# Row-tiled attention with keys and queries in one tile of three places: eight transfers a turn for fourteen, and another order of the sync queue's turn

## What is computed

```python
def attention(query, key, value, mask):         # query is layernorm(x), key and value are ctx
    q = split_heads(query @ Wq.T + bq)           # 16 heads of 8
    k = split_heads(key @ Wk.T + bk)
    v = split_heads(value @ Wv.T + bv)
    scores = einsum('bhqd,bhkd->bhqk', q, k) / sqrt(8)
    scores = where(mask, finfo.min, scores)
    return merge(softmax(scores) @ v) @ Wo.T + bo

x = x + tanh(g_xattn) * attention(layernorm(x), ctx, ctx, mask)
x = x + tanh(g_ffn) * experts(layernorm(x))      # softmax gate less a threshold, gelu, two layers each
```

## Time and profile before

| what | us |
|---|---|
| median of three runs | 675.66 |
| the profiled execution | 676.67 |
| its span, first to last instruction | 674.9 |
| PE busy (share of the span) | 613.6 (91%) |
| DVE busy | 496.8 (74%) |
| ACT busy | 377.8 (56%) |
| POOL busy | 175.8 (26%) |
| mean granted clock of TensorE | 0.944 |

### The profile page before, as it was taken

One profiled execution on the slowest core, in us unless ns is written; L12 is line 12 of the kernel. 1 busy time (PEld: TensorE's weight loads), 2 busy tenths in 40 slices (PEclk: granted clock), 3 DMA queues, 4 the chain that ended last, 5 costly groups with the idle time before them and its releaser, 6 DMA issues.

```text
span 674.9 us, 13858 instructions
## 1 busy us (share of the span) xinstructions
PE 613.6 (91%) x4480; PEld 464.6 (69%) x4480; DVE 496.8 (74%) x926; ACT 377.8 (56%) x620; POOL 175.8 (26%) x223
## 2 busy tenths in 40 slices
PE   5798889889888988749999999999999999999998
PEld 4655556556566655437878878878788788787886
DVE  4447787685766676555888888888888888888886
ACT  2134444454544444517766766767667666676673
POOL 5423333333434223210121221221212212212121
PEclk8769898897988899959999999999999999999999
DMA  5545454454543432004112111111112121111110
GB/s 155 180 132 146 130 150 135 131 152 119 159 122 115 124 120 63 3 1 70 48 48 63 48 47 63 48 47 62 47 48 60 47 62 47 47 62 47 46 63 16
DMA packets 50879, 55.14 MB, mean 82 GB/s; under 512 B 10768, under 2 KB 37264, under 8 KB 50832
## 3 DMA queue, kind: packets, MB, share of 16 engines
q1 hardware_dynamic: 50672, 54.51, 27.9%
q10 hardware_dynamic: 160, 0.00, 0.0%
HBM read 39.16 MB, written 14.81 MB: 80 GB/s over the span
## 4 chain that ended last, share of the span: by engine, by line
PE 73%; SPq 10%; DMA 7%; issue 3%; ACT 3%; DVE 2%; POOL 1%; DVEq 0%; ACTq 0%
PE ps_h L1086 9%; PE ps_y L1066 9%; PE ps_y L1067 9%; PE ps_y L1068 9%; PE ps_h L1088 9%; PE ps_h L1087 9%; DMA mask_words<-in_mask 5%; PE scores L872 4%; SPq L401 3%; PE misc L935 3%; SPq L393 3%; SPq L384 2%; PE scores L890 2%; PE misc L863 2%; PE misc L961 2%
## 5 line engine op out<-in xcount | busy, mean ns | idle before, releaser
L618 ACT ACTIVATE h_sb<-ps_h,b_sb 128x512 f32<-128x512 f32 x256 | 176.3, 690 | 109.0 <-PE ps_h L1088 95.6
L823 DVE TENSOR_TENSOR h_low<-h_sb,h_high 128x512 fp32r<-128x512 f32 x256 | 164.3, 682 | 0.0
L819 DVE CAST h_high<-h_sb 128x512 fp32r<-128x512 f32 x128 | 98.5, 770 | 68.5 <-ACT h_sb L618 68.5
L506 POOL TENSOR_TENSOR yT<-yT,weighted 128x512 f32<-128x512 f32 x54 | 69.7, 1291 | 301.8 <-DVE weighted L811 301.8
L648 DVE TENSOR_REDUCE neg_max<-scores 128x8 f32<-128x1024 f32 x64 | 77.8, 1221 | 50.6 <-PE scores L872 50.5
L1086 PE MATMUL ps_h<-x_high,w_high 128*128 (+1 forms) x256 | 102.9, 402 | 2.3 <-ACT h_sb L618 1.6
L1066 PE MATMUL ps_y<-h_high,w_high 128*128 128x512 f32 x256 | 101.6, 397 | 0.8 <-DVE h_low L823 0.8
L1067 PE MATMUL ps_y<-h_low,w_high 128*128 128x512 f32 x256 | 101.4, 396 | 0.0
L1068 PE MATMUL ps_y<-h_high,w_low 128*128 128x512 f32 x256 | 101.1, 395 | 0.0
L1088 PE MATMUL ps_h<-x_high,w_low 128*128 (+1 forms) x256 | 100.0, 391 | 0.0
L1087 PE MATMUL ps_h<-x_low,w_high 128*128 (+1 forms) x256 | 99.9, 390 | 0.0
(11 more groups left out here) (124 smaller groups left out, 783.0 us busy)
## 6 DMA issues: line engine op xcount, KB each, us to landing
w_row<-w_scratch SPq DMA_DIRECT2D x64, 256.0 KB, 3.1
kq_scratch<-kq_high SPq DMA_DIRECT2D x64, 128.0 KB, 2.6
k_st<-kq_scratch SPq DMA_DIRECT2D x64, 96.0 KB
q_st<-kq_scratch SPq DMA_DIRECT2D x64, 96.0 KB
w_raw<-in_w_ffn SPq DMA_DIRECT2D x16, 256.0 KB, 2.9
kq_scratch<-kq_low SPq DMA_DIRECT2D x32, 128.0 KB, 2.1
ctx_sb<-in_ctx SPq DMA_DIRECT2D x16, 128.0 KB, 2.4
out_y<-y_out SPq DMA_DIRECT2D x7, 256.0 KB, 2.3
```

The costliest lines, as they stand in the source:

```text
L618: nc.scalar.activation(h_sb[:, j % HBUF, :], ps_h[:, j % 4, :], ACT.Gelu_apprx_tanh, bias=b1_sb[:, j:j + 1]).then_inc(h_done, 1)
L819: V.tensor_copy(h_high[:, j % HBUF, :], h_sb[:, j % HBUF, :]).then_inc(high_odd, 1)
L823: V.tensor_tensor(h_low[:, j % HBUF, :], h_sb[:, j % HBUF, :], h_high[:, j % HBUF, :].bitcast(F32), ALU.subtract).then_inc(low2_done, 1)
```

## The change

Keys and queries now lie in one tile `kq_st` with three places (group g in g % 3), each row with keys and queries side by side. One load of 24 x 2048 takes both, so four loads stand for eight. ScalarE and VectorE write four parts into `kq_parts` in the order k_low, q_high, k_high, q_low, so that two neighbours are one combination and one store of 32 x 4 x 512 takes both; with two high stores of 32 x 4 x 256 that makes four stores for six. The bytes are the same. The copies of the max rows, two for each b, stay as they are but for their target.

SP's turn has another order: max rows of b = 1, x, ctx, w_raw, the mask (now of the group after the next, `group_at(it, 2)`), loads of kq, max rows of b = 0, high stores, low stores. The wait for a free place looks three groups back. The second norm's scaling (L712, now L734) moves on VectorE from behind `kq_low` to behind `inT_low`. `headsT` and `x_biased` have one place instead of two, and their writers wait for the group before.

At the start, ctx of group 1 is loaded earlier, six loads of weights and biases (`later_weights`) come behind the first kq loads, group 0's two low stores are issued by ScalarE (`first_low_stores`), the V weights' split (`first_weights`) comes behind group 0's kq parts on both engines, and the nine idle matmuls before group 0's scores become two there and one, two or three at four other points (before group 0's and group 1's kq matmuls, group 0's first max transpose and V's matmuls); the nine at the very start stay.

```diff
-        k_st = sa("k_st", [P, 2, SLABS, GT], F32R)
-        q_st = sa("q_st", [P, 2, SLABS, GT], F32R)
-        kq_high = sa("kq_high", [P, 2, 2, GT], F32R)
-        kq_low = sa("kq_low", [P, 2, 2, GT], F32R)
+        kq_st = sa("kq_st", [P, 3, SLABS, 2, GT], F32R)
+
+        kq_parts = sa("kq_parts", [P, 2, 4, GT], F32R)
...
+            sp.dma_start(ctx_sb[:, 1, :, :], ctx_v[1]).then_inc(ctx_in[1], 16)
             sp.dma_start(wv_raw, a["wvT"]).then_inc(wts_early_in, 16)
...
+            def later_weights():
+
+                sp.dma_start(bo_row[:], a["bo"].partition_broadcast(P)).then_inc(wts_in, 16)
...
+            def rows_of(g, c):
+                return kq_dram[g].rearrange("(r c d) (s x) -> c (d s) r x", r=ROWS, c=3, s=SLABS)[c]
...
-                    for n, c in ((0, 1), (1, 2)):
-                        store(n, c, kq_low[:, u, n, :], g, low_stored[u])
...
+                    if g > 0:
+                        wait_count(sp, mask_done, g - 1)
+                        sp.dma_start(mask_words[:, u, :, :], mask_v[g]).then_inc(mask_in[u], 16)
+                if (g := group_at(it, 1)) is not None:
+                    u = g % 2
...
+                    sp.wait_ge(high_stored[u], g // 2 * 32 + 32)
+                    sp.wait_ge(low_stored[u], g // 2 * 32 + 32)
+                    wait_count(sp, tr_low_full, 2 * (g - 3) + 2)
+                    for r in range(ROWS):
+                        sp.dma_start(kq_st[32 * r:32 * r + 24, g % 3, :, :, :].rearrange("p s n t -> p (s n t)").bitcast(F32),
+                                     kq_dram[g, 24 * r:24 * r + 24, :]).then_inc(kq_in[g % 3], 16)
+                    if g == 0:
+                        later_weights()
+                if (g := group_at(it, 0)) is not None:
+                    misc_wait_read(sp, "max0", g)
+                    wait_count(sp, tr_low_full, 2 * (g - 3) + 1)
...
-                    for n, c in ((0, 0), (0, 2), (1, 0), (1, 1)):
-                        store(n, c, kq_high[:, u, n, :], g, high_stored[u])
+                    for n in range(2):
+                        sp.dma_start(rows_of(g, 0)[:, :, n * GT:(n + 1) * GT], kq_parts[:, u, 2 - n, :].bitcast(F32)).then_inc(high_stored[u], 16)
+                    if g > 0:
+                        misc_wait_read(sp, "kq", g)
+                        for c in (1, 2):
+                            sp.dma_start(rows_of(g, c), kq_parts[:, u, 2 * c - 2:2 * c, :].rearrange("p n t -> p (n t)").bitcast(F32)).then_inc(low_stored[u], 16)
...
+            def first_low_stores():
+
+                rows = kq_dram[0].rearrange("(r c d) (s x) -> c (d s) r x", r=ROWS, c=3, s=SLABS)
+                misc_wait_read(act, "kq", 0)
+                nc.scalar.dma_start(rows[1], kq_parts[:, 0, 0:2, :].rearrange("p n t -> p (n t)").bitcast(F32)).then_inc(low_stored[0], 16)
...
-                    if g >= 2:
-                        misc_wait_full(act, "heads", g - 2)
-                    nc.scalar.activation(headsT[:, u, 0, :], misc[:, bank_of("V0"), 0:2 * P], ACT.Copy).then_inc(misc_read[bank_of("V0")], 1)
+                    if g >= 1:
+                        misc_wait_full(act, "heads", g - 1)
+                    nc.scalar.activation(headsT[:, 0, :], misc[:, bank_of("V0"), 0:2 * P], ACT.Copy).then_inc(misc_read[bank_of("V0")], 1)
...
-                        idle_turns(9)
-                pe.wait_ge(km_in[u], g // 2 * 64 + 64)
-                pe.wait_ge(qm_in[u], g // 2 * 64 + 64)
+                        idle_turns(2)
+                pe.wait_ge(kq_in[g % 3], g // 3 * 64 + 64)
```

More of the change, by code:

```diff
@@ L146, in gated_block @@
         maxT = sa("maxT", [2 * H, GB, S], F32R)
-        headsT = sa("headsT", [P, 2, GB, 2 * P], F32)
+        headsT = sa("headsT", [P, GB, 2 * P], F32)
         sums_r = sa("sums_r", [P, GB * H], F32)
@@ L150, in gated_block @@
         mergedT = sa("mergedT", [P, 2, GT], F32)
-        x_biased = sa("x_biased", [P, 2, GB, D], F32)
+        x_biased = sa("x_biased", [P, GB, D], F32)
         stats2 = sa("stats2", [P, 2, GB, 6], F32)
@@ L358, in body @@
[L358 to L362 removed]
+                        sp.dma_start(kq_st[24 + n::32, g % 3, :, 1, 1 * S:(1 + 1) * S].bitcast(F32), maxT[n * H:(n + 1) * H, 1, :].bitcast(F32)).then_inc(max_in[1][g % 3], 16)
                 if (g := group_at(it, 6)) is not None:
@@ L736, in body @@
                                             ALU.subtract).then_inc(misc_read[bank_of("inputs")], 1)
-                    if g == 0:
-                        first_weights()
+                if (g := group_at(it, -2)) is not None:
+                    u = g % 2
+                    dve.wait_ge(rstd2_done, g + 1)
+                    if g >= 2:
+                        misc_wait_full(dve, "x2T", g - 2)
+                    for b in range(GB):
+                        nc.vector.tensor_scalar(x2n[:, u, b, :], x_all[:, g * GB + b, :],
+                                                mean_var2[:, u, b, 0:1], rstd2[:, u, b:b + 1], ALU.subtract, ALU.mult).then_inc(x2n_done, 1)
                 if (g := group_at(it, -4)) is not None:
@@ L868, in idle_turns @@
                 for _ in range(n):
-                    mm(scores[:, 0, 0:GT], x2T[:, 0, 0:P], x2T[:, 0, :], start=True, stop=True)
+                    mm(scores[:, 5, 0:GT], x2T[:, 0, 0:P], x2T[:, 0, :], start=True, stop=True)
             def natural_mask(r, b, u):
@@ L889, in natural @@
                         rows = slice(32 * r, 32 * r + 24)
-                        mm(scores[:, r, s * S:(s + 1) * S], q_st[rows, u, s, b * S:(b + 1) * S], k_st[rows, u, s, b * S:(b + 1) * S],
+                        mm(scores[:, r, s * S:(s + 1) * S], kq_st[rows, g % 3, s, 1, b * S:(b + 1) * S], kq_st[rows, g % 3, s, 0, b * S:(b + 1) * S],
                            start=(s == 0), stop=False)
@@ L912, in transposed @@
                         rows = slice(32 * r, 32 * r + 26)
-                        mm(scores[:, 2 + r, s * S:(s + 1) * S], k_st[rows, u, s, b * S:(b + 1) * S], q_st[rows, u, s, b * S:(b + 1) * S],
+                        mm(scores[:, 2 + r, s * S:(s + 1) * S], kq_st[rows, g % 3, s, 0, b * S:(b + 1) * S], kq_st[rows, g % 3, s, 1, b * S:(b + 1) * S],
                            start=(s == 0), stop=False)
```

116 lines of the change are left out of this document (43 added, 73 removed).

## The result

The changed kernel takes **641.32 us** (median of 4 runs, 640.2 to 643.27) for 675.09 of the kernel before beside it (4 runs, 673.3 to 677.96): ratio 0.950, 95% interval 0.946 to 0.954. The prediction was 636, 626 to 655. The profiled execution took 640.58, its span 638.7 at a mean clock of 0.975.

A forecast was written before the change was run, and what follows sets the result against it. The sync queue's strict order, not the bytes, was taken as the bottleneck, making TensorE wait and its clock fall. 676.67 - 30.4 (turns) - 7.3 (head) - 2.4 (turns 0 and 1) = 636.6, stated as 636, range 626 to 655.

The forecast's parts named there:

- The turn: Steady turns: 13.6 us of TensorE's own stream plus 0.2 wait, 13.8 each; thirteen turns 178.1 for 208.5, -30.4 us.
- Clock 1.00 with no gap over 1 us: Steady turns: without TensorE gaps over 1 us the clock stays 1.00, where eight of twelve turns showed 0.81 to 0.90.
- The mask, the scaling, the stores: Steady turns: mask wait gone; scaling takes 0.60 us and moves merged by 0.5; stores cost nothing.
- new wait of 0.2 us: Steady turns: the moved scaling delays merged to 14.9, TensorE asks at 14.65, so it waits 0.2 us per turn.
- rival A: Steady turns: max rows of b=0 land late behind the k/q loads; turn 15.7 us, total 661; chance 0.12.
- Rival D: Steady turns: max rows late by L behind slower double loads, turn 13.8+L+1.4, slower than before from L=1.6; chance 0.05.
- The head: Start of the kernel, to group 0's scores: they start at about 21.1 instead of 28.4, -7.3 us.
- scores of group 0 before 22: Head: sign of the forecast being right, group 0's scores matmul starting before 22 us.
- landed by 20.5 to 21: Head: group 0's four k/q loads, issued at about 16.4 to 18.2, have landed by 20.5 to 21 us.
- The idle pairs and the mask's cast: Head: two idle matmul pairs for nine cost 1.3 us; GpSimd's mask cast comes about 1.5 us sooner, at 20.9.
- Ends: 24.5, if loads collide with the deferred weights: Head: late end for the start of group 0's scores, 24.5 us, if k/q loads collide with the deferred weights.
- Turns 0 and 1: First two turns after the head: 27.0 us for 29.4, -2.4; ends 0 and -6.

The follow-up runs named there:

- Experiment 1: Kernel before with only the mask's load moved, from behind the k/q loads to behind w_raw, one group further ahead: 651.69 us, ratio 0.961.
- experiment 2: Changed kernel with the second norm's scaling back at its old place on VectorE: 643.7 us, ratio 0.948.
- after_again: Changed kernel run once more, unchanged, beside other kernels on the same chip: 643.51 us, ratio 0.950 to the kernel before.
- two_places: Changed kernel with two places of the k/q tile instead of three: 690.93 us, ratio 1.017 to the kernel before.
- eight_short: Changed kernel with each k/q load cut at the middle of its 24 rows, eight loads for four: 681.91 us, ratio 1.006.
- eight_late: Changed kernel with x, context and FFN weight loads behind the stores, and k/q loads cut at the middle of their 24 rows: 661.35 us, ratio 0.976.
- experiment 9: Changed kernel with the fill with ones cut in three, a place at a time: 643.91 us, ratio 0.949.
- all_three: Changed kernel with bulk loads behind the stores, the fill place by place, and the value bias on its own semaphore: 636.89 us, ratio 0.942.
- experiment 4: Changed kernel with the max rows of b=0 issued ahead of the k/q loads: 655.52 us, ratio 0.965.

## Why the prediction was right, and where it was not

**The turn: right.** 13.6 for TensorE's own stream plus 0.2 was predicted, 13.67 came, and thirteen turns gave 29.2 for 30.4. The missing 1.2 are turns like that from 51.69 (14.90), where the max rows came 0.9 late and the clock fell to 0.93 and 0.96 in that turn and the next. "Clock 1.00 with no gap over 1 us" was not quite so: this fall followed a wait of 0.90 us, and none followed the wait of 1.03 at 106.25. Experiment 1 shows the cause that the prediction named: the mask load's place in a queue that works in order.

**The mask, the scaling, the stores: right**, but the scaling's 0.5 of VectorE time was never on the path in either direction, as experiment 2 shows. The "new wait of 0.2 us" for merged, one of the signs of being right, exists only in the weight load queue (2.3 us in 8 places).

**Max rows, rival A: the mechanism is real, its size a little over nothing here.** Its sign, TensorE waiting at the transposed scores of b=0, did come, in 3 of the thirteen turns and one before them. The loads were to land "by about 9.5", the max rows at 9 to 10, needed at 10.79. The packets end at 10.1 and 10.0 in the median, and TensorE could use the rows some 0.8 after that (0.7 to 0.9 in the three), so that the room of 1 us was in truth about none; in the turns that waited they were used at 11.2 to 11.9 (106.25 - 94.38 is the longest). That the waits stayed at 2.3 us in these turns is in part luck: the same kernel waits 3.5 us for them in all in this trace and 6.6 us in after_again's, whose execution is 9.4 us longer.

**Rival D's formula**, 13.8 + L + 1.4 a turn, fits where the waits are long: with the mean waits of 1.9 and 1.6 us of two_places and eight_short it gives 17.1 and 16.8, measured 17.4 and 16.8. It said slower than before from L = 1.6 on, and the ratios are 1.017 and 1.006 (the second within the 1% that counts as no change). For small waits it asks too much: 15.9 for eight_late's mean of 0.7, measured 14.6, since the clock fell in only some of its turns.

**The head: the step that failed.** "Group 0's scores at 21.1: -7.3"; it was 25.46 and -2.9. So the sign "scores of group 0 before 22" did not come. Two terms were mis-sized. The fill of three places was not costed at all: 5.18 us for 1.76, worth 1.3 us of the scores' start by experiment 9; it is most of the 2 us by which the last load was issued late (20.18 for 18.2). And the loads "landed by 20.5 to 21", that is 2.3 to 2.8 us after the last issue, were used after 5.3 (20.18 to 25.46), 5.4 with the fill cut (18.99 to 24.40 in all_three) and 5.2 in a full turn of experiment 4, so that the deferred weights behind them need not be the reason. The idle pairs and the mask's cast, which the prediction took as the bound, were done by then. "Ends: 24.5, if loads collide with the deferred weights" was too short too.

**Turns 0 and 1**: 3.2 for 2.4, within its ends. The misses add up: 4.4 in the head and 1.2 in the turns too much, 0.8 here and 0.8 in the rest too little, 4.0 from 636.6 to 640.6. The range held because the turns, 30.4 of the 40.1 us forecast, were right; the head was not.

## What to carry to other kernels

In a queue that works in order, write down for each transfer not only when it is issued but when the packets of the larger transfers ahead of it end: here the small transfer on the critical path landed with the big ones. Take that time from a trace of the same cut, for the same bytes in twice as many loads took 7.0 us for 5.0. A wait saved by one place of one load (here 25 of 29 us) can be found before any regrouping; regrouping then decides how near the next transfer stands to its edge, and beyond that edge, with waits of 1.6 us or more a turn in the mean, a turn cost 1.4 to 1.6 us more than its wait, since the clock fell. Cost the one-time fill of a tile whenever its size is multiplied.

## What was not expected of the hardware

- The issue of a load of 96 KB took 757 ns when each of its 24 rows was taken out in four pieces on both sides, and 364 ns when it was whole rows (363, at least 299, for 12 rows of twice the length). Bytes are equal.
- The same 96 packets of 8 KB took some 0.6 us each in four loads of 24 rows and 0.9 in eight of 12 rows, with 12 in flight in both.
- The second of two max-row transfers of 8 KB took 1.7 us in the chain behind slowly issued loads and 4.4 to 5.8 behind quick ones.
- A fill took 1.76 us for 128x2048 and 5.18 for 128x6144 on VectorE: in these two its time goes with the elements.
- Four row-group loads of 192 KB were used 5.2 to 5.4 us after their last issue, in a full turn (180.49 to 185.65 in experiment 4) as in the head.
- The changed kernel varied more from run to run (641.63 to 649.99 in seven) than the one with the max rows off their edge (636.46 to 639.01 in six).
